# A four-layer gated cross-attention kernel: the local layer's values product turned around, first rows and loads begun a stage ahead, and identity products in TensorE's waits

## The reference

```python
x = x + jnp.tanh(g_xattn[0]) * _L0_xattn_ref(_layernorm(x), ctx, ...)   # local: windows of 16 features
x = x + jnp.tanh(g_ffn[0])   * _L0_ffn_ref(_layernorm(x), ...)          # top-2 of 8 low-rank experts
x = x + jnp.tanh(g_xattn[1]) * _L1_xattn_ref(_layernorm(x), ctx, ...)   # 32 heads, keys of ctx and x
x = x + jnp.tanh(g_ffn[1])   * _L1_ffn_ref(_layernorm(x), ...)          # threshold experts
x = x + jnp.tanh(g_xattn[2]) * _L2_xattn_ref(_layernorm(x), ctx, ...)   # one head
x = x + jnp.tanh(g_ffn[2])   * _L2_ffn_ref(_layernorm(x), ...)          # ternary weights, 8-bit rows
x = x + jnp.tanh(g_xattn[3]) * _L3_xattn_ref(_layernorm(x), ctx, ...)   # 32 heads, 8 key heads
x = x + jnp.tanh(g_ffn[3])   * _L3_ffn_ref(_layernorm(x), ...)          # softmax experts
```

```python
q = _pointwise(Wq, bq, x); k = _pointwise(Wk, bk, cond); v = _pointwise(Wv, bv, cond)
idx = jnp.arange(T)[:, None] + jnp.arange(W)[None, :]          # T = 512, W = 16
dots = jnp.einsum('bhdt,bhdtw->bhtw', qh, k_win) * scale
out = jnp.einsum('bhtw,bhdtw->bhdt', jax.nn.softmax(dots, axis=-1), v_win)
return _pointwise(Wo, bo, out.reshape(b, C, T))
```

## Time and profile before

| | us |
|---|---|
| median of 3 runs | 3506.91 (3504.07 to 3519.98) |
| the profiled execution, its own time | 3514.04 |
| its span, first to last instruction | 3512.1 |
| PE busy | 3332.2 (95%) |
| DVE, ACT, POOL busy | 1829.7, 1467.3, 1058.1 |

### The profile page before, as it was taken

How to read it: one execution, slowest core, us unless ns; L and a number is a source line. 1 busy time by engine, 2 the same in 40 slices (tenths; PEclk the granted TensorE clock), 3 DMA queues, 4 the chain that set the end, 5 groups by cost and what they waited for, 6 DMA issues and landing times. The chain is left out here.

```text
span 3512.1 us, 49665 instructions
## 1 busy us (share of the span) xinstructions
PE 3332.2 (95%) x18879; PEld 2751.2 (78%) x18882; DVE 1829.7 (52%) x3665; ACT 1467.3 (42%) x3294; POOL 1058.1 (30%) x608
## 2 busy tenths in 40 slices
PE   7999989999999999999989895999999999999996
PEld 6888875788888888888875444888788878888885
DVE  4888764333433343333344366655655565555554
ACT  4444422444444444444432354444444444444443
POOL 4333313223323332322221012334333333333323
PEclk8999989999999999999999997999999999999998
DMA  2000011222221221121100301222222212222201
GB/s 101 1 1 1 1 40 36 74 66 61 74 65 61 78 66 60 61 67 61 61 34 1 141 13 72 65 68 67 77 67 66 78 61 73 66 67 67 73 30 55
DMA packets 56655, 199.61 MB, mean 57 GB/s; under 512 B 9088, under 2 KB 9856, under 8 KB 53120
## 3 DMA queue, kind: packets, MB, share of 16 engines
q1 hardware_dynamic: 56448, 196.80, 17.0%
HBM read 192.58 MB, written 4.19 MB: 56 GB/s over the span
## 5 line engine op out<-in xcount | busy, mean ns | idle before, releaser
L1632 POOL TENSOR_TENSOR h_wol<-h_ro,h_woh 128x1024 fp32r<-128x1024 f32 x128 | 313.7, 2451 | 612.2 <-ACT h_woh L1680 612.2
L2114 DVE COPY h_tf<-ps 128x512 f32<-128x512 f32 (+1 forms) x256 | 142.6, 557 | 617.1 <-PE ps L1896 617.0
L1628 POOL TENSOR_TENSOR h_wql<-h_rq,h_wqh 128x1024 fp32r<-128x1024 f32 x128 | 309.0, 2414 | 507.4 <-ACT h_wqh L1675 507.4
L2118 DVE TENSOR_TENSOR h_ol<-ps,h_oh 128x512 fp32r<-128x512 f32 x256 | 177.0, 691 | 527.7 <-ACT h_oh L1733 527.3
L134 PE MATMUL ps<-h_woh,h_oh 128*128 128x512 f32 x1024 | 427.3, 417 | 5.7 <-DVE h_ol L2118 5.7
L134 PE MATMUL ps<-h_Xh,h_wqh 128*128 128x512 f32 x1024 | 414.2, 405 | 2.5 <-ACT h_qf L1729 1.4
L136 PE MATMUL ps<-h_woh,h_ol 128*128 128x512 f32 x1024 | 404.8, 395 | 0.0
L135 PE MATMUL ps<-h_wol,h_oh 128*128 128x512 f32 x1024 | 404.3, 395 | 0.0
L136 PE MATMUL ps<-h_Xh,h_wql 128*128 128x512 f32 x1024 | 402.3, 393 | 0.0
L135 PE MATMUL ps<-h_Xl,h_wqh 128*128 128x512 f32 x1024 | 399.9, 390 | 0.0
L1783 ACT ACTIVATE h_ex<-ps,h_mx 128x128 f32<-128x128 f32 x512 | 180.9, 366 | 269.7 <-DVE h_mx L2154 269.7
(11 more groups left out here) (291 smaller groups left out, 6629.1 us busy)
## 6 DMA issues: line engine op xcount, KB each, us to landing
h_rq<-in_L_Wq SPq DMA_DIRECT2D x128, 512.0 KB, 3.5
h_ro<-in_L_Wo SPq DMA_DIRECT2D x128, 512.0 KB, 3.5
h_rk<-in_L_Wkv SPq DMA_DIRECT2D x47, 512.0 KB, 3.5
h_craw<-in_ctxT SPq DMA_DIRECT2D x7, 1024.0 KB, 6.1
cnat<-in_ctx SPq DMA_DIRECT2D x4, 1024.0 KB, 8.2
t_craw<-in_ctxT SPq DMA_DIRECT2D x4, 1024.0 KB, 7.2
t_cn<-in_ctx SPq DMA_DIRECT2D x4, 1024.0 KB, 7.9
out_rows<-x SPq DMA_DIRECT2D x16, 256.0 KB, 2.2
```

The costliest lines, as they stand in the source:

```text
L1628: nc.gpsimd.tensor_tensor(wql[:, par], rq[:, par], f(wqh[:, par]), ALU.subtract).then_inc(m["p_wq"], 1)
L1632: nc.gpsimd.tensor_tensor(wol[:, par], ro[:, par], f(woh[:, par]), ALU.subtract).then_inc(m["p_wo"], 1)
L2114: nc.vector.tensor_copy(tf[:], ps[:, TBK, 0:PT]).then_inc(m["v_t"], 1)
L2118: nc.vector.tensor_tensor(by_head(ol), ps[:, AB, :].rearrange("p (b h t) -> p b h t", h=2, t=S), f(by_head(oh)), ALU.subtract).then_inc(m[ ...
```

## The change

1. **Local stage.** `values` is turned around: the spread-out values are stationary (64 columns, `vx`), the turned shares move (64 columns), 16 matmuls per step in place of 4, and the result lands with features already in columns, two halves of the PSUM partitions. `pick`, its mask and the DVE product L499 are gone; `own_heads` on DVE, once every two steps, keeps the right head out of four by 4 operations with a column of 4 flags. The scaling of the shares moves from DVE to POOL (`shares`), between POOL's mask products. `sc`, `ex`, `pr` and the sums get two buffers. PE's order becomes `turn(g-2)`, `scores(g)`, projections, `values(g-2)`. `output` becomes 4 matmuls of 256 columns, and the score bank is given free after the addition and no longer after the maximum.
2. **First rows ahead.** `FirstRows` does the first group's rows of mixture 0, mixture 1 and the last mixture inside the stage before (in its last tile, or at the last group's second key head), with one `xn` for all stages. The text stage's first three loads are issued in mixture 1.
3. **Products that nothing reads.** `occupy(bank, n)` multiplies the identity by itself, 512 columns, `n` times into a bank whose content is not needed. It stands at the start of the local stage (there with a tile of ones), in its first two steps, in the last group of the text stage, and at the ends of the stages.

```diff
+        xn = sb("xn", [P, NT, D])
...
+        def occupy(bank, n):
+            for _ in range(n):
+                nc.tensor.matmul(ps[:, bank, :], ident[:], ident[:].unsqueeze(1).broadcast_to((P, 4, P)), start=True, stop=True)
...
+                        def masked_queries(j, heads):
+                            if heads[0] == 0:
+                                pool.wait_ge(a_q, j + 1)
+                                wait(pool, s_s, NQ * (j - 1))
+                            for h in heads:
                                 last = nc.gpsimd.tensor_tensor(
                                     qx[:, j % 2, :, h, :], qs[:].rearrange("p (n t) -> p n t", t=TB),
                                     hmask[:, h:h + 1].unsqueeze(2).broadcast_to((P, D // TB, TB)), ALU.mult)
-                            last.then_inc(p_qx, 1)
+                            if heads[-1] == HEADS0 - 1:
+                                last.then_inc(p_qx, 1)
+                        def shares(g):
+                            pool.wait_ge(v_rc, g + 1)
+                            wait(pool, s_t, g - 1)
+                            nc.gpsimd.tensor_tensor(pr[:, g % 2], ex[:, g % 2],
+                                                    rc[:, g % 2].unsqueeze(3).broadcast_to((P, 2, NB, KW)),
+                                                    ALU.mult).then_inc(p_pr, 1)
+                        masked_queries(0, range(HEADS0))
+                        for g in range(STEPS):
+                            j, n = g // NQ, g % NQ
+                            if g >= 1:
+                                shares(g - 1)
+                            if j + 1 < NTILE and n < 3:
+                                masked_queries(j + 1, (range(0, 2), range(2, 5), range(5, 8))[n])
+                        shares(STEPS - 1)
...
-                            pe.wait_ge(v_pr, g + 1)
+                            pe.wait_ge(p_pr, g + 1)
...
-                            wait(pe, v_om, g)
+                            if g % 2 == 0:
+                                wait(pe, v_oc, g // 2 - 1)
                             for b in range(2):
                                 for q in range(2):
-                                    last = nc.tensor.matmul(
-                                        ps[:, AB + b, q * 256:(q + 1) * 256], at[:, 2 * b + q, :],
-                                        vx[:, j % 2, 2 * n + q, b].rearrange("p n o -> p (n o)"), start=True, stop=True)
+                                    for r in range(2):
+                                        col = (4 * b + 2 * q + r) * S
+                                        for hh in range(2):
+                                            half = slice(S * hh, S * hh + S)
+                                            last = nc.tensor.matmul(
+                                                ps[half, ZB + g % 4, col:col + S],
+                                                vx[:, j % 2, 4 * n + 2 * q + b, hh, 2 * r:2 * r + 2].rearrange("p n o -> p (n o)"),
+                                                at[:, 2 * b + q, half], start=True, stop=True)
                             last.then_inc(s_av, 1)
...
-                        def pick(g):
...
+                            pe.wait_ge(v_oc, 2 * (j + 1))
                             pe.wait_ge(a_vx, min(j + 3, NTILE))
                             if j == 0:
-                                pe.wait_ge(l_wo, 16 * 2)
-                            nc.tensor.matmul(ps[:, PB, :], wbd["o"][:], oc[:], start=True, stop=True).then_inc(s_wo, 1)
+                                pe.wait_ge(l_wo, 16 * 4)
+                            for n in range(2):
+                                for b in range(2):
+                                    last = nc.tensor.matmul(
+                                        ps[S * b:S * b + S, PB, 256 * n:256 * n + 256], wo2[:, n],
+                                        oc[:, j % 2, :, b].rearrange("p n c t -> p n (c t)"), start=True, stop=True)
+                            last.then_inc(s_wo, 1)
...
+                        pe.wait_ge(c_t, 1)
+                        for _ in range(8):
+                            nc.tensor.matmul(ps[:, ZB + 3, :], tmp[:, 0:P], tmp[:], start=True, stop=True)
                         pe.wait_ge(l_w, 16 * 6)
                         pe.wait_ge(l_c, 16 * len(loads))
                         queries(0)
                         keys(0)
                         values_of_context(0)
+                        occupy(ZB + 3, 2)
                         value_rows(0)
+                        occupy(ZB + 3, 3)
                         for j in range(NTILE):
                             for n in range(NQ):
                                 g = NQ * j + n
+                                if g >= 2:
+                                    turn(g - 2)
                                 scores(j, n)
                                 if j + 1 < NTILE:
                                     if n == 0:
...
                                         value_rows(j + 1)
                                 if n == 3 and j:
                                     output(j - 1)
-                                if g >= 1:
-                                    turn(g - 1)
                                 if g >= 2:
-                                    pick(g - 2)
-                                if g >= 1:
-                                    values(g - 1)
-                        turn(NQ * NTILE - 1)
-                        pick(NQ * NTILE - 2)
-                        values(NQ * NTILE - 1)
-                        pick(NQ * NTILE - 1)
+                                    values(g - 2)
+                                else:
+                                    occupy(ZB + 3, 2)
+                        for g in (STEPS - 2, STEPS - 1):
+                            turn(g)
+                            values(g)
                         output(NTILE - 1)
+                        occupy(ZB, 2)
...
+                        def shares_sum(g):
+                            dve.wait_ge(a_e, g + 1)
+                            own(nc.vector.tensor_reduce(st[:, 1], ex[:, g % 2], AX_X, ALU.add))
+                            wait(dve, p_pr, g - 1)
+                            nc.vector.reciprocal(rc[:, g % 2], st[:, 1]).then_inc(v_rc, 1)
+                        def own_heads(k):
+                            dve.wait_ge(s_av, 2 * k + 2)
+                            wait(dve, s_wo, k // 2 - 1)
+                            z = ps[:, ZB + 2 * (k % 2):ZB + 2 * (k % 2) + 2, :].rearrange("p a (c h t) -> p (a c) h t", h=HH, t=TB)
+                            o = oc[:, k // 2 % 2, 2 * (k % 2):2 * (k % 2) + 2].rearrange("p n b c t -> p (n b c) t")
+                            own(nc.vector.tensor_scalar(o, z[:, :, 0], hm4[:, 0:1], None, ALU.mult))
+                            for h in range(1, HH):
+                                last = nc.vector.scalar_tensor_tensor(o, z[:, :, h], hm4[:, h:h + 1], o, ALU.mult, ALU.add)
+                                if h < HH - 1:
+                                    own(last)
+                            last.then_inc(v_oc, 1)
...
-                                own(nc.vector.tensor_tensor(sc[:], sv, band[:].unsqueeze(1).unsqueeze(1).broadcast_to(
-                                    (P, 2, NB, KW)), ALU.add))
-                                nc.vector.tensor_reduce(st[:, 0], sc[:], AX_X, ALU.max).then_inc(v_s, 1)
+                                nc.vector.tensor_tensor(sc[:, g % 2], sv, band[:].unsqueeze(1).unsqueeze(1).broadcast_to(
+                                    (P, 2, NB, KW)), ALU.add).then_inc(v_s, 1)
                                 dve.wait_ge(v_s, g + 1)
-                                nc.vector.tensor_tensor(sc[:], sc[:], bc(st[:, 0]), ALU.subtract).then_inc(v_sub, 1)
+                                own(nc.vector.tensor_reduce(st[:, 0], sc[:, g % 2], AX_X, ALU.max))
+                                nc.vector.tensor_tensor(sc[:, g % 2], sc[:, g % 2], bc(st[:, 0]), ALU.subtract).then_inc(v_sub, 1)
+                                if g >= 1:
+                                    shares_sum(g - 1)
...
-                                dve.wait_ge(a_e, g + 1)
-                                own(nc.vector.tensor_reduce(st[:, 1], ex[:], AX_X, ALU.add))
-                                own(nc.vector.reciprocal(st[:, 2], st[:, 1]))
-                                wait(dve, s_t, g)
-                                nc.vector.tensor_tensor(pr[:], ex[:], bc(st[:, 2]), ALU.mult).then_inc(v_pr, 1)
-                                if g >= 1:
-                                    masked(g - 1)
+                                if g % 2 == 0 and g >= 4:
+                                    own_heads(g // 2 - 2)
...
+        class FirstRows:
+
+            def stats(self, dve):
+                self.own = Own(dve, self.own_sem)
+                self.norm[0](self.own, 0)
+            def root(self, act):
+                self.norm[1](act, 0)
```

(37 more changed lines are left out.)

241 lines of the change are left out of this document (126 added, 115 removed).

## The result

The changed kernel takes 3495.6 us (median of 20 runs, 3485.4 to 3502.0), the one before 3507.4 (20 runs). The ratio is 0.9955, with an interval of 0.9945 to 0.9965: faster by about 12 us, or 0.5%, where 60 were forecast. The profiled execution (3486.5 us, span 3484.5) is one of the shortest of its kernel, and that of before was 7 us over its median, so the two profiles differ by 27.6 us. The parts are read from these two profiles; for the whole the medians count.

What follows compares the result with a forecast made beforehand. PE was taken to bound the local stage, then a loop through DVE and POOL. Terms 33 + 5 + 5 + 9 + 2.5 + 8 - 2 = 60.5 us made 3453.5 profiled, 3447 median; range 3412 to 3488.

Steps and rivals of the forecast that it cites:

- What bounds the kernel, and the loop: Local stage: PE bounds it before; after, a loop from scores through DVE, POOL and turn sets 6.75 us a step.
- The step that failed: Local loop: steps shrink from 7.03 to 6.75 us, 0.28 each, gaining 16.5 us over 59 steps.
- a rival of 0.10: Local loop: PE's waits let its clock fall, half the steps 4.6 us longer, +138, total 3585 us; chance 0.10.
- Values: Local step: the turned-around values, 32 records, take 2.0 us, between a lower end of 0.9 and an upper of 3.4.
- The first rival: Local step: values cost 0.106 us a record, perhaps with drains, adding 18 to 27 us, total 3470; chance 0.17.
- DVE and POOL: Local loop, rival: they collide, subtraction up to 1.58 us for 0.69, +26 us, total 3473; chance 0.08.
- Start: Local stage: first scores at 25.0 us, scores of tile 1 at 50.5 for 62.98, 12.5 us earlier.
- Boundaries: Between stages: rows and loads ahead and a held clock gain 5, 5, 9, 2.5 and 8 us, less 2.
- the row of heads 3: Heads 3 to the last mixture's weights: forecast 7 us shorter, with rows ready ahead and the clock.
- Mixture 0 and the text stage: Stage starts: local to mixture 0 gains 5 us with weights as bound; mixture 1 to text gains 9.
- Heads 1: Heads stage: rows made there ahead of the softmax cost 1 us, or 5 if their cover fails.
- the three gentler rivals: Whole kernel: dear values 3470 us (0.17), DVE and POOL colliding 3473 (0.08), between-stage gains staying away 3474 (0.06).

Runs made afterwards that it cites:

- e5_fill_half: Changed kernel plus identity products ahead of turn in each local step (2, in step 1 of a tile 1): 3459.7 us, ratio 0.9863.
- e9_shares_twice: e5_fill_half with POOL's product of the shares issued twice in each step, the first into an unread buffer: 3541.7 us, ratio 1.0089.
- e10_shares_dve: e5_fill_half with the shares back on DVE behind the reciprocal, in place of POOL: 3474.1 us, ratio 0.9903.
- e2_behind: Changed kernel with PE's order scores(g), values(g-3), turn(g-2), then projections, so turn stands behind the scores: 3384.0 us, ratio 0.9642.
- e1_fill: Changed kernel plus identity products ahead of turn in each local step (4, in step 1 of a tile 2): 3514.4 us, ratio 1.0015.
- e8_values_twice: e2_behind with the 32 records of values issued twice, same results into the same places: 3394.4 us, ratio 0.9673.
- e4_noident: Changed kernel without identity products at the ends of the stages and in the text tail; those at the local start stay: 3488.5 us, ratio 0.9937.
- e3_bounds: Changed kernel with the local stage of the kernel before, so only the changes outside that stage remain: 3497.8 us, ratio 0.9965.

## Why the prediction was wrong

- **What bounds the kernel, and the loop:** right. 6.71 to 6.94 us a step were worked out, 6.75 taken, 6.63 measured (e5_fill_half); e9_shares_twice and e10_shares_dve move it by +1.01 and -0.40 as the chain says, and e2_behind opens it.
- **The step that failed** is "The gain per step is therefore 7.03 - 6.75 = 0.28 ... over 59 steps 16.5 us". It prices every step at the full clock. The sum knew that PE would have 5.7 us of work in 6.75 (about 4.5 in fact, since values and output were cheaper); it put the clock into a rival of 0.10, "against" which stood one stretch of 3 us at 2.35 busy. The 0.65 us without work there say nothing on a wait of 2.3 us that comes nearly every step. The rows to ask were those where PE had waited for as long: 3.03 us ahead of the first scores, which then ran at the lower clock, and 2.21 us in the third step, behind which the clock stood at 0.50 for 20 us. Here are the row behind that wait and the stretch after it, from the kernel before:

```profile
43.28 1.24 PE L312 MATMUL ps<-ident,vw 128*128 128x128 f32 x8 [2.21 <-ACT vw L424]
```

```profile
44.00:64.00 20.00, 20.00 (x82) 18.56 (x80) 7.33 (x11) 6.92 (x9) 0.00 (x0) 0.50 0.00 1
```

The term came out at +9.1 where -16.5 were forecast: -23.3 for the loop (59 x 6.63 = 391.2) and +32.5 for the clock, of which e5_fill_half gives back 30.8.
- **That rival** had the right mechanism and the wrong size: "half of the steps are hit", at 4.6 us each, 3585. Hit were 13 in 59 by 1.4 to 2 us, and 15 by less. The price of 4.6 us took a step wholly at 1.2 GHz and PE's work at 5.7 us. Here most falls cover only a part of a step or a little more: by the granted clock they last 3.4 to 13.7 us in the loop, and the one at its end 30.7. What ends a fall stays open. It isn't PE's being busy alone: in the kernel before PE was busy for all of the 20 us shown above, and the clock stayed at 0.50.
- **Values:** 2.0 us taken, 1.08 measured (207.06 to 208.14 in e2_behind; 0.034 us a record, 0.031 doubled), between the lower end of 0.9 and mine. The first rival falls: no drain is to be seen. By this PE had 0.9 us a step less to do, and its waits were longer by so much. `output` took 0.92 us for 1.8, likewise (its records in e1_fill, 259.32 to 260.24). e8_values_twice shows what a cheap product can mean for the clock: with the 32 records doubled the clock is 1.00 for 0.96, and the 2048 more records cost 10 us.
- **DVE and POOL:** right that they don't meet; the rival's price (0.69 to 1.51) came true in e10_shares_dve.
- **Start:** right, 13.4 for 12.5 (first scores at 24.34 for 25.0, then 5.32 and three times 6.63). It is not the same in every run: with the same start e4_noident gains 10.6, since one of its first steps takes 7.02 us for 5.32.
- **Boundaries:** the second term that was too large. By the medians e3_bounds, which has them alone, gains 12 us (5 to 20) where 27.5 were forecast: about 15 of the 48 us that the whole change falls short. The profiles are kinder: for the seven rows of the table behind the last scores 31.5 us were forecast, drain included, and 23.3 measured, while eleven other kernels with the changed ends have 13 to 23 less there than the kernel before. What holds in all of them is the gain ahead of mixture 1's weights (6.4 to 6.6 us for 13.4, where 5 were forecast). That the row of heads 3 met its forecast (7.6 for 7) is luck: with the same ends the others have 1283.5 to 1289.7 us there, 0.2 to 6.4 less than before. Mixture 0 and the text stage came out too low. There the weights arrive piece by piece over 3.7 us (496.81 to 500.46), and mixture 1, whose weights do the same, takes up part of the text's gain.
- **Heads 1** became 3.7 us longer, where 1 was charged. Its start shows about 3 of them: PE waits 4.43 us for DVE, 1.0 more than before, and the next ten products take 0.44 us each for 0.23, at the lower clock. This isn't the price of the rows made there, for e3_bounds has the same rows in its heads 1, which takes 1221.7 us, 0.4 over before. Its wait at this place is 3.04 us (the last row), and no fall follows:

```profile
604.92 0.80 PE L141 MATMUL ps<-h_Xh,h_wkh 128*128 128x512 f32 x1 [4.43 <-DVE h_Xl L2203]
605.52 0.63 PE L142 MATMUL ps<-h_Xl,h_wkh 128*128 128x512 f32 x1
...
624.57 0.50 PE L141 MATMUL ps<-h_Xh,h_wkh 128*128 128x512 f32 x1 [3.04 <-DVE h_Xl L2165]
```

- **The range** began at 3412 and ended at 3488, since it took in the three gentler rivals and left the clock out. With the clock held the change gives 3459.7 us (e5_fill_half), 13 over the forecast, which is about what the boundaries fell short.

## What to carry to other kernels

On an engine whose clock falls behind waits, as PE's does here, a wait has a price of its own: before counting a gain from less work on PE, see what PE will wait for, how long and how often, and look in the trace for waits of that size and the clock behind them. Where a loop through other engines sets the step, move the waiting instruction behind independent work first (here four transposes behind the scores: 112 us); fill what is left with products that nothing reads, sized by the records in the trace and not by the instructions, and fill every wait of the pattern, not one. Work that is taken off a waiting engine can come back as a lower clock.

## What was not expected of the hardware

- 2048 extra records of 64 x 64 (64 steps of 32) cost 10 us in all by the medians, about 37 by the plain tiles; the clock rose from 0.96 to 1.00.
- Work that fills one wait in four lowers nothing: 3504.0 us, against 3495.6 with none of the four filled and 3459.7 with all. Where the clock has already fallen, the filling itself is on the path (steps of 8.66 to 9.21 us, for 8.0 to 8.3 in the same places of the changed kernel).
- The clock stayed at its lower level for 20 us in which PE was busy without a gap (the kernel before, 44 to 64 us).
- A record of `values`, 64 stationary and 64 moving columns in one half of the array, takes 0.031 to 0.034 us, against 0.106 of the records of the scores with 128 stationary columns and as many moving.
